# Attention scores in four row quarters, a new order of a pair on every engine, and GpSimd dividing the second batch

## The reference

```
q, k, v = (xn @ wq + bq), (xn @ wk + bk), (xn @ wv + bv)   # 16 heads of 32 features
scores = einsum('bhqd,bhkd->bhqk', q, k) / sqrt(32)
attn = softmax(scores, axis=-1)
out = einsum('bhqk,bhkd->bhqd', attn, v)
x = residual + (out @ wo + bo)
```

## Time and profile before

| what | value |
|---|---|
| median of 3 runs | 2042.7 us (2040.06 to 2044.53) |
| the profiled execution's own time | 2038.54 us |
| its span in the profile | 2036.8 us |
| PE busy | 96% of the span |
| attention phase, first to last matmul | 769.9 to 1308.8 us |
| one pair in the steady loop | 31.97 us |

### The profile page before, as it was taken

How to read it: one execution, slowest core, us unless ns; L and a number is a source line. 1 busy time by engine, 2 the same in 40 slices (tenths; PEclk the granted TensorE clock), 3 DMA queues, 4 the chain that set the end, 5 groups by cost and what they waited for, 6 DMA issues and landing times. The chain is left out here.

```text
span 2036.8 us, 31437 instructions
## 1 busy us (share of the span) xinstructions
PE 1964.9 (96%) x10194; PEld 1616.5 (79%) x10194; DVE 1229.1 (60%) x2060; ACT 754.0 (37%) x2232; POOL 414.1 (20%) x525
## 2 busy tenths in 40 slices
PE   6899999999999998999999999799999999999999
PEld 4678888887888887888888888578888788788887
DVE  6677777777777656777777777564352525245322
ACT  3222333322232325777777777431221212121211
POOL 4223333322222222222122222110010101011100
PEclk8999999999999998999999999899999999999999
DMA  8455444445444435777777777631020201112000
GB/s 301 150 164 175 154 149 149 136 158 165 164 154 150 149 104 153 209 226 220 216 236 209 225 223 217 207 102 62 22 83 1 83 26 57 48 37 72 11 21 21
DMA packets 237151, 275.60 MB, mean 135 GB/s; under 512 B 16172, under 2 KB 161160, under 8 KB 237064
## 3 DMA queue, kind: packets, MB, share of 16 engines
q1 hardware_dynamic: 222824, 231.38, 36.0%
q0 software_dynamic: 12080, 38.87, 6.3%
q10 hardware_dynamic: 2160, 4.20, 0.6%
HBM read 166.38 MB, written 91.23 MB: 126 GB/s over the span
## 5 line engine op out<-in xcount | busy, mean ns | idle before, releaser
L617 PE MATMUL mlp_y<-weights,mlp_h 128*128 128x512 f32 x1536 | 380.4, 398 | 10.7 <-DVE mlp_h L854 9.3
L594 PE MATMUL ffn_m<-xn,weights 128*128 128x512 f32 x1536 | 374.4, 394 | 9.2 <-issue 6.9
L617 PE MATMUL ffn_y<-weights,ffn_h 128*128 128x512 f32 x1536 | 377.4, 395 | 1.5 <-DVE ffn_h L854 1.4
L594 PE MATMUL mlp_m<-xn,weights 128*128 128x512 f32 x1536 | 371.2, 392 | 5.6 <-DVE xn L842 5.6
L617 PEld LDWEIGHTS mlp_y<-weights,mlp_h 128*128 128x128 f32 x1536 | 289.4, 189 | 82.9 <-issue 9.2
L594 PEld LDWEIGHTS ffn_m<-xn,weights 128*128 128x128 f32 x1536 | 291.4, 190 | 74.3 <-issue 11.2
L594 PEld LDWEIGHTS mlp_m<-xn,weights 128*128 128x128 f32 x1536 | 290.2, 189 | 69.7 <-DVE xn L842 6.0
L617 PEld LDWEIGHTS ffn_y<-weights,ffn_h 128*128 128x128 f32 x1536 | 288.2, 188 | 70.8 <-DVE ffn_h L854 2.3
L730 ACT ACTIVATE ffn_g<-ffn_m,vecs 128x512 f32<-128x512 f32 x128 | 88.3, 690 | 561.1 <-PE ffn_m L594 561.1
L852 DVE CAST ffn_h<-ffn_g 128x512 fp32r<-128x512 f32 x128 | 57.6, 450 | 386.3 <-ACT ffn_g L730 385.5
L730 ACT ACTIVATE mlp_g<-mlp_m,vecs 128x512 f32<-128x512 f32 x128 | 88.1, 688 | 373.2 <-PE mlp_m L594 364.9
(11 more groups left out here) (130 smaller groups left out, 2044.3 us busy)
## 6 DMA issues: line engine op xcount, KB each, us to landing
turned_probs<-att_probs SPq DMA_DIRECT2D x64, 512.0 KB, 3.1
x_tiles<-x SPq DMA_DIRECT2D x98, 256.0 KB, 2.9
x<-x_tiles SPq DMA_DIRECT2D x96, 256.0 KB, 3.5
mlp_bias<-gate_bias_rows POOLq DMA_DIRECT2D x64, 256.0 KB, 4.0
att_kdiag<-xn SPq DMA_DIRECT2D x128, 128.0 KB, 2.5
probsT_room<-turned_probs SPq DMA_DIRECT2D x64, 256.0 KB, 3.8
x_tiles<-turned_probs SPq DMA_DIRECT2D x64, 256.0 KB, 3.8
turned_squares<-mlp_xhat SPq DMA_DIRECT2D x62, 256.0 KB, 3.2
```

The costliest lines, as they stand in the source:

```text
L594: last = nc.tensor.matmul(m1_ps[:, c % 2, :], st.tiles[0](a, k, c), xn[:, parity, b, k, :], start=s == 0, stop=s == len(steps) - 1)
L617: last = nc.tensor.matmul(y_ps[:, tile, :], h[:, c % 2, a, tile * P:(tile + 1) * P], st.tiles[1](b, c), start=c == 0 and s == 0, stop=c == ...
```

## The change

- Scores. `kdiag`, its DMAs and its wait are gone. A batch's scores are one call: 48 matmuls, each of 32 rows (one head's features, a row quarter of the array) and 128 columns, four neighbours in the four quarters and in four different PSUM banks. Both halves' row maxima wait for the whole call, and the call waits until all 16 heads of the batch before have been exponentiated.
- Products go round the three banks of `bank_ps`; the projection of a first batch no longer uses a bank of the scores.
- The order of a pair is new on PE, ACT, DVE, POOL and SP. `keys_queries(n, 0)` moves to the start of its own step, the projection of the second batch moves to the step after next.
- The second batch's probabilities are divided by POOL, both halves. ACT's division and one on DVE are gone. `piece_low` moves from DVE to POOL.

```diff
-            def diag(n, tile):   # four DMAs kst -> kdiag, gone with kdiag
...
+            def divide(n, e):
+                heads = slice(HALF * e, HALF * (e + 1))
+                pool.wait_ge(inv_done, 4 * n + 2 + e + 1)
+                half = probs[:, e, :, :, :].rearrange("p c h i -> p h c i")
+                nc.gpsimd.tensor_tensor(half, half, inv[:, heads].unsqueeze(2).unsqueeze(3).to_broadcast([P, HALF, NSQ, SQ]),
+                                        ALU.mult).then_inc(pool_divided, 1)
...
-                for m in (2 * e, 2 * e + 1):
-                    last = product(score_bank(m), [(q[:, a, m, tile * P:(tile + 1) * P], kdiag[:, b, m, :]) for a, b in MUL_HI_LO])
+                if not is_first(row):
+                    pe.wait_ge(exp_done, 2 * row)
+                for m in range(KC):
+                    for a, b in MUL_HI_LO:
+                        for j in range(HPC):
+                            rows = slice(j * HD, (j + 1) * HD)
+                            last = nc.tensor.matmul(s_ps[:, j * KC + m, :], q[rows, a, m, tile * P:(tile + 1) * P], kst[rows, b, m, tile * P:(tile + 1) * P],
+                                                    start=(a, b) == MUL_HI_LO[0], stop=(a, b) == MUL_HI_LO[-1])
                 last.then_inc(scores_done, 1)
```

More of the change, by code:

```diff
@@ L1336, in weigh @@
                     pe.wait_ge(probsT_loaded[e], 32 * (row + 1))
[L1337 to L1342, removed]
+                for m in range(KC):
+                    for j in range(HPC):
+                        head, (e, u) = m * HPC + j, divmod(j, 2)
+                        last = nc.tensor.matmul(o_ps[j * HD:(j + 1) * HD, m, :], v[:, tile, head * HD:(head + 1) * HD],
+                                                probsT[e][:, u, :, m * SQ:(m + 1) * SQ], start=True, stop=True)
                 last.then_inc(out_done, 1)
@@ L1365, in pair_step @@
                 if is_pair(n):
[L1366 to L1370, removed]
+                    keys_queries(n, 0)
+                    keys_queries(n, 1)
+                    keys_queries(n, 2)
+                    keys_queries(n, 3)
+                    keys_queries(n, 4)
                     keys_queries(n, 5)
@@ L1374, in pair_step @@
                     turn(n + 1, 0)
+                if is_pair(n):
+                    keys_queries(n, 7)
+                if is_turned(n + 1):
+                    turn(n + 1, 1)
+                if is_pair(n - 2):
+                    project(n - 2, 1)
+                if is_pair(n):
+                    scores(n, 0)
+                if is_pair(n - 1):
+                    weigh(n - 1, 0)
+                if is_pair(n):
+                    values(n, 0)
+                    values(n, 1)
                 if is_pair(n - 1):
@@ L1378, in pair_step @@
                     value_bias_product()
[L1379 to L1387, removed]
                 if is_pair(n - 1):
@@ L1390, in pair_step @@
                 if is_pair(n):
[L1391 to L1396, removed]
+                    scores(n, 1)
             schedule(pe, first, pair_step)
@@ L1458, in exponentials @@
                     last.then_inc(exp_done, 1)
[L1460 to L1468, removed]
             def piece_high(n):
@@ L1618, in pair_step @@
             def pair_step(n):
+                if is_pair(n - 1):
+                    row_max(n - 1, 1, 0)
+                    turn_probs(n - 1, 0, 1)
                 if is_pair(n):
@@ L1621, in pair_step @@
                 if is_pair(n - 1):
-                    divide(n - 1, 1, 0)
+                    row_max(n - 1, 1, 1)
                 if is_pair(n):
                     kq_low(n, 1)
+                if is_turned(n + 1):
+                    stats(n + 1, 0)
+                if is_pair(n):
+                    kq_low(n, 2)
+                if is_pair(n - 1):
+                    invert(n - 1, 1, 0)
+                if is_pair(n):
+                    kq_low(n, 3)
+                if is_turned(n + 1):
+                    normalise(n + 1, 0)
+                    stats(n + 1, 1)
+                if is_pair(n):
+                    kq_low(n, 4)
+                if is_pair(n - 1):
+                    invert(n - 1, 1, 1)
+                if is_pair(n):
+                    kq_low(n, 5)
+                if is_turned(n + 1):
+                    normalise(n + 1, 1)
                 if is_pair(n - 1):
```

223 lines of the change are left out of this document (97 added, 126 removed).

## The result

| kernel | median of the runs | against before |
|---|---|---|
| before | 2043.0 us (2040.1 to 2044.8) | |
| after | 2034.2 us | 0.9956 (0.9945 to 0.9968) |

After is 0.44% faster; I had forecast 2064 us, slower. The time lies in the range, the sign is wrong. One of the six executions of after took 10810.8 us, for a reason that is not known; the ratio goes by the other five, which took 2031.4 to 2037.4. The profiled execution took 2031.38 us (before 2038.54), its span is 2029.6.

The account below looks back on a forecast made before the run. PE bounded the old pair (31.97 us); a 32.6 us loop through POOL and DVE would bound the new. Fifteen steps (+10), first step (+2), last pair (+7), clock (+2): +21, 2059.5 profiled, 2064 median; range 2003 to 2100.

Parts of the forecast that it names:

- Scores, 6.40 gone and 3.2 come: PE, per pair: old score calls of 6.40 us go, two new calls of 1.6 come; PE's work becomes 28.8 us.
- the low end that I gave for that: PE, a call of scores if the row quarters don't overlap: 4.3 us, of 4.3 to 5.8; chance 0.10.
- POOL and DVE shut each other out, `normalise` finds POOL inside: DVE: `normalise` waits for POOL's tensor_tensors, always finding a division running; 2.3 to 2.5 us instead of 0.5.
- I take 2.45, nearest to the twofold: POOL's division: 2.45 us, near twice the 512-element `add_bias` (2.58 at most); floor 1.23, upper bound 3.8.
- the prediction's own slope: Loop of a steady pair: each further 0.1 us of a POOL division adds 0.2 us.
- in turns: End of step, POOL and DVE alternate: `add_bias` 1.29, `divide` 1.15, `add_bias` 1.2, `x_low` 0.55; 4.2 us.
- First step, +2: Attention's first step: `scores(0, 1)` waits for 16 exponentials, `piece_high` now first on ACT waiting for its load; +2 us.
- Last pair, +7: Last pair: both POOL divisions in the open (2.4 us), a `normalise` behind each, row maxima start later; +7 us.
- Clock, +2: PE's granted clock drops after a few of the new idle stretches of 1 to 1.6 us; +2 us.
- The sum of the attention: Whole attention: steady steps, first step, last pair and clock together; +21 us.
- Rival 4: `x_low` gets in before the second `add_bias`: 1.1 us less a pair, 31.5; 2046 us; chance 0.10.
- Rival 1: Divisions are covered and PE stays the bound at 28.8 us plus small waits a pair; 2003 us; chance 0.13.

Follow-up runs that it names:

- The two moves: Changed kernel with each `normalise` ahead of the `invert` releasing POOL's division, and POOL's two `add_bias` separated and moved clear of DVE's `divide` and `x_low`: 1985.1 us, 0.9715.
- the run with the second instruction: Changed kernel with a second POOL tensor_tensor (160 elements of scratch) behind each division, before it counts as done: 2032.1 us, 0.9961.

## Why the prediction was wrong

Two steps failed. The price of POOL's division was taken too high, 2.45 us where it measured 1.90, which makes 16.5 of the 20 us by which the attention came out shorter than forecast. And the code behind the attention was put at nothing, where it gave 9.4 us and with them the sign. By item:

- **Scores, 6.40 gone and 3.2 come:** right. A call cost 1.49 against 1.6, PE's work 28.7 against 28.8. Quarter after quarter it would be 4.4, near the low end that I gave for that. By TensorE: Matmul & The Clock Gate of the Trainium skill, section LDWEIGHTS, a load of 32 rows takes as long as one of 128, and by its Part 3 matmuls in different row groups overlap; the trace agrees with both (a load of 32x128 is recorded with 186 ns, one of 128x128 with 188).
- **POOL and DVE shut each other out, `normalise` finds POOL inside:** right, twice a pair, for the 1.9 us of the division.
- **"I take 2.45, nearest to the twofold":** the term that was mis-sized. It took 1.90, inside its bounds of 1.23 and 3.8, under the 2.2 at which the forecast's own range began. By the prediction's own slope that is 2 x 0.55 = 1.1 a pair, 32.6 - 1.1 = 31.5, measured 31.42. With a full operand of 512 elements in place of 8 inverses spread over 128 each, POOL took 2.39, near my 2.45: the twofold of `add_bias` held for that instruction. What makes the division cheaper, the spread operand or the order in which it goes through `probs`, is open, since that run changed both. GPSIMD Engine Reference of the Trainium skill, section 3.1, has 4497 ns for a tensor_tensor of 2048 elements; half of it, an estimate of 2.25, is 6% under the 2.39; it has no figure for an operand that is spread.
- **"in turns", 4.2 for two `add_bias`, `divide` and `x_low`:** the sum held (1018.83 to 1022.97: 4.1), the order did not. DVE was not let in between the two `add_bias`.
- **First step, +2:** it took 1.7 us less. The wait for 16 exponentials, for which the +2 stood, did not come: the second call begins right behind the matmuls before it (PE's timeline below), and the wait of 2.24 us in the earlier trace rows is gone.
- **Last pair, +7:** measured +7.3, the size partly by luck. Of its two `normalise` only the first found POOL's division inside and took 2.11, the second took 0.50. The two moves, with POOL dividing as before, take 4.9 of the 7.3 away, and without POOL's two divisions, for which the prediction had 2.4, nothing more goes. In the changed kernel itself, without the moves, this was not tested.
- **Clock, +2:** measured 5 (four of the steady pairs, 1.27 each).
- **The sum of the attention:** 21 us predicted. 15 x 1.1 = 16.5 of it is the division, 3.7 the first step, some 2 waits that only before has, against 3 more for the clock. That leaves 2; the trace has 1.3, the timed runs 0 to 3.
- **Rival 4 (`x_low` gets in before the second `add_bias`):** its 31.5 a pair is what came, but not by its mechanism: DVE was not let in there, and the pair is short by the division.
- **What the prediction left out:** that a change of PE's program in the attention moves the code behind it. This alone made the sign: 9.4 us in the trace, 0.5 to 0.6% in the timed runs, shown by giving it to the kernel before and by taking a part of it from after. The prediction could have read the four "issue" waits and the return of the loop in before's trace; it could have counted the instructions only with the changed program at hand.
- **Rival 1 (PE stays the bound):** its end was real, 28.7 a pair, but the change as made does not reach it. It took two moves in the order.

PE's timeline of after in the first step:

```profile
788.54 9.89 PE L1279 MATMUL att_banks<-weights,xn 128*128 128x512 f32 x36
798.36 1.56 PE L1309 MATMUL att_s<-xn 32*128 32x128 f32 x48
```

Open: which place in a block decides, beyond that a loop begun at 5 or 168 was never fetched anew, at 192 once of two times, at 208, 216 and 229 always; and whether the attention's own change costs a microsecond or nothing.

## What to carry to other kernels

Before a gain or loss of half a per cent is put down to an edit, compare the phases that the edit does not touch, and look at the instruction packets of the page and at the returns of long loops; a few idle instructions ahead of such a loop can be worth more than the edit. Where two engines shut each other out, it is the order that counts: an instruction put ahead of the one that releases the other engine costs nothing, put behind it it costs the other's whole length (`normalise`, 0.55 us against 1.9). And when work is taken from the engine that bounds a loop, sum the loop through the others as well: here 3.1 us a pair were there to be had, and two waits behind POOL held back nearly all of them.

## What the runs showed of the hardware

- PE fetches its program in blocks of 16 KB. A loop of 1582 instructions that began 5 or 168 into a block ran its second and third round with no fetch at all; begun at 208, 216 or 229 it was fetched anew after each return, and its three rounds took 2.4, 4.8 and 10.9 us longer. Begun at 192 it was fetched anew once, which cost 4.1, so the cost does not simply grow with the place. Runtime: NRT & Kernel Launch of the Trainium skill, section Instruction fetch mechanics, gives PE 128 KiB in blocks of 16, eight blocks, and lets a branch stall whose target lies outside a window of two. The loop that touched seven blocks and never fetched lies within the eight blocks; it does not agree with the two. That a loop over eight was fetched anew does not follow from eight blocks alone.
- A POOL tensor_tensor of 1024 elements took 1.90 us with an operand spread from 8 values, 2.39 with one of 512 elements read twice and the first operand taken in larger pieces.
- Between two instructions of POOL that stood back to back, DVE was let in once (a tensor_scalar, behind the division, in the run with the second instruction) and not the other time (a tensor_tensor, between two `add_bias`). What decides is not shown.
- Matmuls of 32 rows and 128 columns: 0.09 us each one after the other, 0.031 in four quarters.
